# Last stage of a fused attention and mixture-of-experts kernel: groups of 4, 8, 8, 8, 4 tiles, residual rows kept on chip and added by Pool, plain stores

## What is computed

```python
x = content                                    # (4, 1024, 256) float32, 4096 tokens
x = x + layernorm(attention(layernorm(x), Wq, Wk, Wv))      # 16 heads of 16
x = x + layernorm(experts(layernorm(x), router_w, w_fc, w_proj))
# experts: softmax over 8 logits, the best 2, their weights scaled to sum 1,
# out += weight_e * (gelu(x @ w_fc[e]) @ w_proj[e])
# layernorm: (x - mean) / sqrt(var + 1e-5), over the 256 columns
```

## Time and profile before

| | us |
|---|---|
| median of 3 runs | 1625.13 |
| profiled execution | 1626.82, span 1625.1 |
| last scatter issued by Pool | 1582.54 |
| loads of expert_out start | 1586.40 |
| first statistics | 1590.31 |
| last output DMA issued by Pool | 1616.80 |

### The profile page before, as it was taken

The page is one execution under the profiler, slowest core; times in us unless marked ns, Lnnn a source line. Parts: engine busy times, 40 slices in busy tenths (PEclk is TensorE's granted clock), DMA queues, the critical chain, the costliest instruction groups (busy, mean ns, idle before and its releaser), DMA issues.

```text
span 1625.1 us, 31177 instructions
## 1 busy us (share of the span) xinstructions
PE 1455.0 (90%) x9750; PEld 836.1 (51%) x9751; DVE 1026.3 (63%) x1770; ACT 771.8 (47%) x1650; POOL 612.1 (38%) x711
## 2 busy tenths in 40 slices
PE   5988999999999899989999986389999999999990
PEld 3551233333333233323333243289999999999980
DVE  4769777777888788878888977723323233233324
ACT  2330577777777677767777785211111111111114
POOL 5332334543444334533444432123333333333332
PEclk9995899999999999999999998589999999999995
DMA  3569122022220222022213153262222222222229
GB/s 113 172 164 276 40 40 40 10 31 40 40 40 8 35 40 40 15 27 40 40 23 70 53 182 142 45 183 34 39 33 38 39 33 39 34 37 39 32 30 210
DMA packets 87629, 105.07 MB, mean 65 GB/s; under 512 B 11648, under 2 KB 70912, under 8 KB 87520
## 3 DMA queue, kind: packets, MB, share of 16 engines
q1 hardware_dynamic: 69664, 80.80, 21.5%
q0 software_dynamic: 17856, 22.89, 8.9%
HBM read 64.70 MB, written 38.96 MB: 64 GB/s over the span
## 4 chain that ended last, share of the span: by engine, by line
PE 61%; DVE 15%; issue 13%; ACT 4%; POOL 3%; DMA 2%; DVEq 1%; SPq 0%; POOLq 0%; ACTq 0%
PE ps L1153 16%; PE ps L1163 15%; PE ps L1008 10%; DVE negmax L1443 9%; PE ps L980 8%; PE ps L1094 8%; ACT wfc L868 2%; POOL x L668 2%; PE ps L973 2%; PE ps L1081 1%; DVE x L1348 1%; PE ps L1142 1%; ACT wfc L911 1%; DVE wfc L1454 1%; DMA arena<-in_L_ffn_w_proj 1%
## 5 line engine op out<-in xcount | busy, mean ns | idle before, releaser
L1443 DVE TENSOR_REDUCE negmax<-ps 128x1 f32<-128x1024 f32 x512 | 605.9, 1216 | 123.8 <-PE ps L1094 121.3
L868 ACT ACTIVATE wfc<-ps 128x512 f32<-128x512 f32 x768 | 436.6, 595 | 171.2 <-PE ps L980 162.7
L889 ACT ACTIVATE yx<-ps 128x512 f32<-128x512 f32 x142 | 84.8, 597 | 440.6 <-PE ps L1153 440.6
L1153 PE MATMUL ps<-yx 128*128 128x128 f32 x2272 | 270.3, 278 | 4.1 <-DMA arena<-in_L_ffn_w_proj 3.4
L1153 PEld LDWEIGHTS ps<-yx 128*128 128x128 f32 x2272 | 269.7, 195 | 8.3 <-DMA arena<-in_L_ffn_w_proj 3.6
L1163 PE MATMUL ps<-arena,yx 128*128 x1136 | 256.8, 379 | 0.0
L731 POOL TENSOR_TENSOR wfc<-wfc,causal 128x512 f32<-128x512 f32 x128 | 162.6, 1270 | 249.6 <-ACT wfc L868 181.7
L1094 PE MATMUL ps<-arena 96*128 96x512 bf16 x704 | 231.5, 413 | 9.6 <-DVE negmax L1443 4.0
L759 POOL DMA_INDIRECT expert_out<-yx,rt x71 | 112.6, 1586 | 318.3 <-DVE yx L1576 315.3
L1163 PEld LDWEIGHTS ps<-arena,yx 128*128 128x128 f32 x1136 | 210.4, 190 | 25.7
L980 PE MATMUL ps<-arena 120*128 120x512 bf16 x528 | 203.3, 392 | 12.8 <-ACT wfc L868 0.4
(11 more groups left out here) (177 smaller groups left out, 1364.7 us busy)
## 6 DMA issues: line engine op xcount, KB each, us to landing
arena<-qk_parts SPq DMA_DIRECT2D x132, 128.0 KB, 5.9
qk_parts<-x SPq DMA_DIRECT2D x32, 384.0 KB, 2.6
arena<-in_L_ffn_w_proj SPq DMA_DIRECT2D x8, 1024.0 KB, 8.6
wfc<-in_L_ffn_w_fc SPq DMA_DIRECT2D x16, 512.0 KB, 7.5
wfc<-qk_parts SPq DMA_DIRECT2D x60, 128.0 KB, 6.1
expert_out<-rt SPq DMA_DIRECT2D x3, 1408.0 KB, 12.0
yx<-in_L_attn_content SPq DMA_DIRECT2D x8, 512.0 KB, 3.9
x<-in_L_attn_content SPq DMA_DIRECT2D x1, 4096.0 KB, 25.5
```

The source lines that it names most:

```text
L868: nc.scalar.activation(et_sb[b % NET][:, hl, :], bk(ebank(c, g)), ACT.Exp).then_inc(s_expB, 1)
L889: nc.scalar.activation(hidT[s][:, 4 * hf:4 * hf + 4, :], bk(1 + hf).rearrange("p (c t) -> p c t", c=4), ACT.Gelu).then_inc(s_ge, 1)
L1153: ins = nc.tensor.matmul(bk(1 + hf)[:, c * P:(c + 1) * P], w1[s][:, kc * FF + (4 * hf + c) * P:kc * FF + (4 * hf + c + 1) * P], xsT[:, kc, :],
L1443: nc.vector.tensor_reduce(negmax[:, hl % 2, i:i + 1], ps[:, 2 * (k % 2):2 * (k % 2) + 2, :], AX.XY, ALU.max, negate=True).then_inc(s_max, 1)
```

## The change

The 32 tiles of the last stage are cut into `ENDS`: 4, 8, 8, 8 and 4 tiles. Statistics, variance, root, reciprocal and bias exist once per tile in their own columns of a free buffer (part of `yx`), so nothing is reused between groups. VectorE takes the first tile's statistics of the next group ahead of the group's scales, so that it has work while ScalarE takes the root; ScalarE takes the next group's root ahead of its own last tile. Each applied tile steps the semaphore. Pool adds `x1` to tiles 0 to 29, one instruction of 128 x 256 for each, VectorE adds to tiles 30 and 31. SP stores each four finished tiles with a plain DMA. The early stores of `x1` and the adding DMAs go.

```diff
+        ENDS = ((0, 4), (4, 12), (12, 20), (20, 28), (28, 32))
+        ON_DVE = 2
...
 # SP
-            for g in range(TT // TPC):
-                sp.wait_ge(s_add, x2_done(g))
-                sp.dma_start(out_t[:, g * TPC:(g + 1) * TPC, :], x1[:, g * TPC:(g + 1) * TPC, :]).then_inc(s_x1o, 16)
...
+            for q in range(TT // TPC):
+                sp.wait_ge(s_po, min(TPC * (q + 1), TT - ON_DVE))
+                if q == TT // TPC - 1:
+                    sp.wait_ge(s_pd, ON_DVE)
+                sp.dma_start(out_t[:, q * TPC:(q + 1) * TPC, :], yv[:, q * TPC:(q + 1) * TPC, :]).then_inc(s_out, 16)
 # Pool
-            pool.wait_ge(s_x1o, 16 * G)
-            for q in range(G):
-                pool.wait_ge(s_ap, q + 1)
-                pool.dma_start(out_t[:, q * TPC:(q + 1) * TPC, :], yv[:, q * TPC:(q + 1) * TPC, :],
-                               accum_op=ALU.add).then_inc(s_out, 16)
+            for t in range(TT - ON_DVE):
+                pool.wait_ge(s_ap, t + 1)
+                pool.tensor_tensor(yv[:, t, :], yv[:, t, :], x1[:, t, :], ALU.add).then_inc(s_po, 1)
 # ScalarE
-            for q in range(TT // TPC):
-                root_y(q)
-                apply_y(q)
+            root_y(0)
+            for q, (a, b) in enumerate(ENDS):
                 act.wait_ge(s_nm, q + 1)
+                for t in range(a, b):
+                    if t == b - 1 and b < TT:
+                        root_y(q + 1)
+                    nc.scalar.activation(yv[:, t, :], yv[:, t, :], ACT.Identity,
+                                         scale=rstd_e[:, t:t + 1], bias=negm_e[:, t:t + 1]).then_inc(s_ap, 1)
 # VectorE
             def spread(q):
+                a, b = ENDS[q]
+                for t in range(a + (q > 0), b):
+                    bn_e(t)
...
+                if b < TT:
+                    bn_e(b)
...
-            for q in range(NQ):
+            for q in range(len(ENDS)):
                 spread(q)
-                if q:
-                    scales(q - 1)
-            scales(NQ - 1)
+                scales(q)
+            for t in range(TT - ON_DVE, TT):
+                dve.wait_ge(s_ap, t + 1)
+                nc.vector.tensor_tensor(yv[:, t, :], yv[:, t, :], x1[:, t, :], ALU.add).then_inc(s_pd, 1)
```

More of the change, by code:

```diff
@@ L193, in sandwich @@
         yv = wfc[:, 0:TT * D].rearrange("p (t d) -> p t d", d=D)
+        assert o <= 7680
+        stats_e = ym[:, 7680:7680 + 6 * TT].rearrange("p (t s) -> p t s", s=6)
+        mv_e = ym[:, 7872:7872 + 2 * TT].rearrange("p (t s) -> p t s", s=2)
+        std_e, rstd_e, negm_e = (ym[:, 7936 + TT * s:7936 + TT * (s + 1)] for s in range(3))
+        ENDS = ((0, 4), (4, 12), (12, 20), (20, 28), (28, 32))
+        ON_DVE = 2
         negm = sb("negm", [P, 2, TPC])
@@ L300, in sandwich @@
         s_ap = sem("s_ap")
-        s_x1o = sem("s_x1o")
+        s_po = sem("s_po")
+        s_pd = sem("s_pd")
         s_out = sem("s_out")
@@ L904, in root_y @@
             def root_y(q):
+                a, b = ENDS[q]
                 act.wait_ge(s_var3, q + 1)
-                nc.scalar.activation(std[:, q % 2, :], mv[:, q % 2, :, 1], ACT.Sqrt).then_inc(s_std3, 1)
-            def apply_y(q):
+                nc.scalar.activation(std_e[:, a:b], mv_e[:, a:b, 1], ACT.Sqrt).then_inc(s_std3, 1)
+            root_y(0)
+            for q, (a, b) in enumerate(ENDS):
                 act.wait_ge(s_nm, q + 1)
[L910 to L913, removed]
-            for q in range(TT // TPC):
-                root_y(q)
-                apply_y(q)
+                for t in range(a, b):
[3 more added lines that the diff above has]
+                                         scale=rstd_e[:, t:t + 1], bias=negm_e[:, t:t + 1]).then_inc(s_ap, 1)
             act.wait_ge(s_warm, 4)
@@ L1598, in _, with bn_e @@
                 mix(t, t % 2)
-            NQ, CF = TT // TPC, 2 * TPC
+            n_cf = [0]
+            def bn_e(t):
+                if t % TPC == 0:
+                    dve.wait_ge(s_yl[t // TPC], 16)
+                    nc.vector.memset(pause[:, :], 0.0)
+                nc.vector.bn_stats(stats_e[:, t, :], yv[:, t, :]).then_inc(s_cf, 1)
+                n_cf[0] += 1
             def spread(q):
[L1604 to L1607, removed]
+                a, b = ENDS[q]
+                for t in range(a + (q > 0), b):
+                    bn_e(t)
+                dve.wait_ge(s_cf, n_cf[0])
@@ L1608, in spread @@
                 nc.vector.memset(pause[:, :], 0.0)
[L1609 to L1612, removed]
+                for t in range(a, b):
+                    nc.vector.bn_aggr(mv_e[:, t, :], stats_e[:, t, :]).then_inc(s_cf, 1)
+                n_cf[0] += b - a
@@ L1614, in scales @@
+                dve.wait_ge(s_cf, n_cf[0])
+                nc.vector.tensor_scalar(mv_e[:, a:b, 1], mv_e[:, a:b, 1], EPS, None, ALU.add).then_inc(s_var3, 1)
+                if b < TT:
+                    bn_e(b)
             def scales(q):
+                a, b = ENDS[q]
                 dve.wait_ge(s_std3, q + 1)
-                wait_pos(dve, s_ap, q - 1)
-                nc.vector.reciprocal(rstd[:, q % 2, :], std[:, q % 2, :]).then_inc(s_rs3, 1)
+                nc.vector.reciprocal(rstd_e[:, a:b], std_e[:, a:b]).then_inc(s_rs3, 1)
@@ L1618, in scales @@
                 dve.wait_ge(s_rs3, 2 * q + 1)
-                nc.vector.scalar_tensor_tensor(out=negm[:, q % 2, :], in0=mv[:, q % 2, :, 0], scalar=-1.0,
-                                               in1=rstd[:, q % 2, :], op0=ALU.mult, op1=ALU.mult).then_inc(s_rs3, 1)
+                nc.vector.scalar_tensor_tensor(out=negm_e[:, a:b], in0=mv_e[:, a:b, 0], scalar=-1.0,
+                                               in1=rstd_e[:, a:b], op0=ALU.mult, op1=ALU.mult).then_inc(s_rs3, 1)
                 dve.wait_ge(s_rs3, 2 * q + 2)
-                nc.vector.tensor_tensor(negm[:, q % 2, :], negm[:, q % 2, :], shift[:, q * TPC:(q + 1) * TPC],
-                                        ALU.subtract).then_inc(s_nm, 1)
+                nc.vector.tensor_tensor(negm_e[:, a:b], negm_e[:, a:b], shift[:, a:b], ALU.subtract).then_inc(s_nm, 1)
```

## The result

The changed kernel takes 1619.27 us (median of 8 runs, 1617.09 to 1621.5); the kernel before, run beside it, 1624.45 (8 runs, 1622.45 to 1625.83). The ratio is 0.9967, 95% interval 0.9956 to 0.9978: 5.4 us less, between 3.6 and 7.1. The forecast was 3.4 less. The direction was right; the size was not, and neither of its two terms came out: the last stage gave more than its 2.5, and the place in the middle didn't give its 0.9.

A forecast was written before the change was run, and what follows sets the result against it. The prediction took the last stage's ScalarE and VectorE loop plus a 6.4 us landing as the bound. Tail 2.5 and middle 0.9 made 3.4 us less: 1625.13 to 1621.7, range 1619.2 to 1625.6.

The forecast's parts named there:

- its two terms: Last stage 2.5 us less at the tail, experts' start 0.9 us less; together 3.4 us less.
- the place in the middle: Experts' start: without early stores weights land sooner, VectorE's copy is late next, 0.9 us saved.
- What bounds the kernel before: Last stage: a ScalarE and VectorE loop, 2.81 us per group, then one adding DMA landing of 6.4 us.
- The start of the stage: Last stage: first apply at 1593.4, 1.4 us earlier; group 1's root at 1596.85, after eight combines of 0.8 us.
- Pool's adds set the end: Last stage: Pool's adds, pitch 0.685 us, are slower than ScalarE's 0.52 per tile; 26 adds take 17.8 us.
- Where Pool's run begins: Group 1's second bias operation waits for tile 3's add, so Pool's run of 26 begins at 1599.1.
- The turns: VectorE and Pool alternate operations; VectorE waits up to 0.7 us each, Pool loses 0.45 plus 0.3 us.
- That rival: VectorE shut out while Pool has a tile: Pool idles 1.2 us per boundary, whole 1625.5 to 1626.0; chance 0.13.
- The rival by which Pool isn't disturbed: Last stage: Pool is quicker or undisturbed, ends at 1616.3, 1.35 us earlier, whole 1620.4; chance 0.14.
- The lock that is held by whoever starts first: Skill's rule, not adopted: VectorE's final adds would hold Pool 0.42 us each, end some 0.5 us later.
- The last store: SP's plain store of tiles 28 to 31 lands in 3.0 us, then 1.9 us of program end follow.
- both good rivals: Pool quicker or undisturbed (1620.4, chance 0.14) and the low clock in the middle ending sooner (1620.2, chance 0.11).

The follow-up runs named there:

- adds and plain stores alone: Kernel before without early stores, with Pool's and VectorE's adds and SP's plain stores, old groups and order kept: 1625.21 us, ratio 1.0003.
- The late wait: Changed kernel with TensorE's wait for the second weights moved behind the second block's first product: 1617.55 us, ratio 0.9963.
- both mendings: Changed kernel with five adds on VectorE and TensorE's later wait for weights: 1615.4 us, ratio 0.9942; also with the last store in two: 1616.73, 0.9946.

## Why the prediction was right or wrong

Three terms of the tail were mis-sized, all to the same side: the start of Pool's run (1.1 us), its pitch (0.4) and the end of the program behind it (0.6). The 0.9 us of the middle had a cause that the runs don't have. And the reading of what bounds the kernel before was wrong.

**What bounds the kernel before: wrong.** It read 1594.77 to 1614.43 as a loop of ScalarE and VectorE, with one landing behind it. The loop is there, but the DMA engines, at some 190 GB/s and a share of 1.23 for the adding DMAs, were full beside it; speeding up the loop alone gave nothing (38.7 and 38.7). The rows I quoted showed the loads' rate of 351; the share of the stretches after 1600 I didn't weigh. The sum was spared, since it went from a last issue and a landing and both were true as marks; but the landing of 6.4 us was no fixed latency: it grew to 10.6 when the DMAs were issued sooner, and fell to 3.4 without the adding. What one adding DMA takes by itself no run shows; the shortest landing of one was 5.9.

**The start of the stage: right, forecast 0.4 too late.** First apply 6.9 us after the loads' start (forecast 7.0), root of group 1 at 10.1 (forecast 10.45). Eight combines took 0.6, not 0.8.

**Pool's adds set the end: right.** Record 0.738 us (forecast 0.726), pitch 15.06 / 22 = 0.685 up to the last four, just as forecast, and with those (1613.14 - 1594.99) / 26 = 0.70, where the sum had 0.685 and 0.75 us of losses, together 0.71.

**Where Pool's run begins: the step that made half of the miss.** Forecast 12.7 us after the loads' start, measured 11.6. I let the second bias operation of group 1 wait for the add of tile 3; it had started 0.10 us before that add (1594.11 against 1594.21) and took its 0.17 as if alone, as both hang on the same root by ways of nearly the same length. So Pool went from tile 3 to tile 4 without a pause. From here and the quicker combines come 1.1 us, from the pitch 0.4. The last store was issued 29.8 us after the loads' start, forecast 31.3.

**The turns: right for VectorE, too dear for Pool.** The second bias operation took 0.64 at the later boundaries, epsilon 0.40 to 0.61; the two final adds of VectorE 1.52 for both. The first bias operation, also with two inputs, took 0.17 even so. VectorE was never shut out, although Pool's adds have no gap between them. That rival falls. Pool lost nothing that shows at the three boundaries (22 adds at 0.685), where the sum had 0.45, and 0.37 by the two final adds, where it had 0.3. The rival by which Pool isn't disturbed had its end at 1616.3, 29.9 us after the loads' start; measured are 29.8. It was nearer than the forecast, though not for its reason: VectorE's operations didn't slip through, they waited. The lock that is held by whoever starts first has a case for it in the bias operation of group 1, and one against it in VectorE's adds: Pool's slowest add lost 0.19, where the lock would take 0.42.

**The last store: landing right, program end wrong.** Landing 2.9, forecast 3.0; but from the store's issue to the end of the span 4.3 us passed, forecast 4.95. The 1.9 us of program end behind a landing, the last term of the tail, stand behind the last landing in the three kernels where Pool issues the output DMAs and in no other. The end came 4.33 us after Pool's last add instead, 0.6 sooner than forecast. Together the tail lost 4.55 us, forecast 2.5: the difference is 1.1 and 0.4 from Pool's run and 0.6 from here.

**The middle: wrong.** Forecast 0.9 us; the wait for the weights didn't shrink. I took the DMA engines' bytes as shared between the loads and the stores; the landing is the same with and without them, so the stores cost the loads nothing that shows. From Pool's first gather to the third block's product the profile of before has 25.4 us (1051.96, above, to 1077.31) and the changed kernel's 24.5 (1049.88 to 1074.36), which looks like the 0.9 forecast. It is luck: with the stores put back the stretch is 24.1, and in the kernel with adds and plain stores alone, which has no early stores, 25.3. The first product took 6.21 us before and 5.26 after the change, as the granted clock stayed at 0.50 for its first 5 us before and for its first 3 us after. Nor was VectorE's copy late next: it ended at 1062.97, 2.5 us before the landing. In the trace of before it ended only 0.9 us ahead of the weights, as the first product there was held at a lower clock for longer. The late wait shows what was to be had in this place: a stretch shorter by 4.1 us in its own profile, by 1.4 and 1.6 in those of the two kernels with both mendings.

**The rest.** 4.55 of some 5.2 to 5.4 us are in the tail. The remainder is within the scatter of the stages before it: the first gather went out between 1047.8 and 1052.0 us in these profiles, with no relation to what was changed.

**The range.** Its lower end was to be both good rivals together; they come to 1621.7 - 1.35 - 1.5 = 1618.85, and I wrote 1619.2.

## What to carry to other kernels

Two parts that are each worth nothing can be worth 4.5 us of tail together: the adding DMAs hid what the order gave, and the old order hid what the adds gave. Before a loop is called the bound, read the DMA share beside it, and compare it with the share at which plain transfers run; a landing that grows when the DMAs are issued sooner is a queue. Ask what the end of the program really follows: here it was Pool's last add, and splitting the last store was an experiment on something that set nothing. And where an engine waits for data, look whether its next instruction reads them at all: moving the wait past one product took its 4.5 us off the path, though the runs don't resolve what that alone gave.

## What the runs showed of the hardware

- DMAs that add onto DRAM moved 174 to 198 GB/s at a share of 1.21 to 1.24; the same DMAs without adding moved 228 at a share of 0.66, in the stretch shown, and landed in 3.4 us, where the adding one, under the same order of work, took 8.4 in the median (5.9 to 10.6). The issue on Pool fell from 1.27 to 0.75 us.
- Pool's add of 128 x 256 float32 took 0.738 us (0.712 to 0.926), back to back at 0.685, with VectorE's small operations beside them too; an add of VectorE of the same size beside them made one 0.19 longer.
- After Pool's last add the span went on for 4.32 to 4.33 us in all nine kernels with such adds, whatever the last store did.
- VectorE's second bias operation, with two on-chip inputs, took 0.64 to 0.65 beside back-to-back adds of Pool, 0.16 alone; the first, 0.2 us ahead of it, 0.17 in the change, 0.38 and 0.48 in two other kernels. An add of 128 x 256 on VectorE took 0.47 to 1.03 where Pool's adds ran on, 0.41 with Pool idle. That agrees with the part of the Trainium skill, "SBUF — State Buffer", section "Who interferes with whom", by which a VectorE instruction with two SBUF inputs contends with a GpSimd instruction that reads SBUF. Epsilon, with one input, waited too: 0.38 to 0.70 beside the adds, 0.17 alone.
- The second of two loads of 1 MB landed 9.3 to 10.1 us after issue, with or without 4 MB of stores queued behind it. In the changed kernel nearly all of its bytes had moved 2 us before TensorE was released (1065.43). From 1063.5 on, SP's queue (`q1`) moved 33 packets more, 0.03 MB at 22 GB/s, with 4.8% of the 16 engines' time, the last at 1064.85. That is as if one DMA engine of the 16 finished alone; why one was late stays open.

```profile
q1 hardware_dynamic: 33, 0.03, 4.8%
```
